# Two sums over all tokens in a linear attention: VectorE adds the token tiles in pairs first, TensorE makes four products for each sum

## The reference, cut to what matters

```
qkv = x @ qkv_w.T + qkv_b                 # 1024 tokens, 16 heads of 8
q, k = sigmoid(q), sigmoid(k)
k_sum = k.sum(tokens)                     # first sum over all tokens, with q_sum
q_sum = q.sum(tokens)
sink_incoming   = 1 / sum((q + EPS) * (k_sum + EPS))
source_outgoing = 1 / sum((k + EPS) * (q_sum + EPS))
k_so_sum = (k * source_outgoing).sum(tokens)   # second sum, with q_si_sum
q_si_sum = (q * sink_incoming).sum(tokens)
conserved_sink   = sum((q + EPS) * (k_so_sum + EPS)) + EPS
conserved_source = clip(sum((k + EPS) * (q_si_sum + EPS)) + EPS, -1, 1)
...
out = (q * sink_incoming) @ (k.T @ (v * softmax(conserved_source) * n)) * sigmoid(conserved_sink)
```

## Time and profile before

| | |
|---|---|
| median of three runs | 2540.83 us |
| the profiled execution | 2537.11 us |
| its span in the trace | 2535.4 us |
| mean granted TensorE clock | 0.962 of full speed |
| TensorE, VectorE, ScalarE, GpSimd busy | 91%, 77%, 65%, 32% of the span |
| first sum (L1850): matmul records, busy | 128, 35.8 us (eight sequences) |
| second sum (L1857): matmul records, busy | 128, 29.8 us |

### The profile page before, as it was taken

One profiled execution on the slowest core, in us unless ns is written; L12 is line 12 of the kernel. 1 busy time (PEld: TensorE's weight loads), 2 busy tenths in 40 slices (PEclk: granted clock), 3 DMA queues, 4 the chain that ended last, 5 costly groups with the idle time before them and its releaser, 6 DMA issues.

```text
span 2535.4 us, 64762 instructions
## 1 busy us (share of the span) xinstructions
PE 2310.6 (91%) x25503; PEld 1658.4 (65%) x25503; DVE 1949.4 (77%) x3307; ACT 1660.4 (65%) x3050; POOL 804.1 (32%) x653
## 2 busy tenths in 40 slices
PE   5989989899898998989989899899998999988998
PEld 3667556675666766667657676566665766666765
DVE  6778877788778887687876878868778687786876
ACT  4866558665586656775577755768457684585845
POOL 2221442315324052241522315313253033530334
PEclk8999999999999999999999999999899999999989
DMA  7110221103111121111211112111121102211022
GB/s 252 51 42 2 96 65 43 42 8 116 39 43 42 44 85 35 47 38 45 88 33 48 34 60 77 35 47 31 63 77 36 46 27 76 69 38 48 18 80 63
DMA packets 99123, 141.34 MB, mean 56 GB/s; under 512 B 11523, under 2 KB 60620, under 8 KB 98316
## 3 DMA queue, kind: packets, MB, share of 16 engines
q1 hardware_dynamic: 90636, 120.41, 15.2%
q0 software_dynamic: 8192, 16.79, 2.3%
HBM read 101.84 MB, written 31.13 MB: 52 GB/s over the span
## 4 chain that ended last, share of the span: by engine, by line
PE 72%; DVE 14%; ACT 6%; issue 6%; POOL 1%; SPq 0%; DVEq 0%; DMA 0%; POOLq 0%; ACTq 0%
PE ps L1727 11%; PE ps L1556 11%; PE ps L1749 10%; PE ps L1764 10%; PE ps L1563 6%; PE ps L1638 5%; DVE neg_max L1225 3%; PE ps L1660 3%; PE ps L1513 2%; DVE ffn L1356 2%; ACT probs L833 2%; PE ps L1577 2%; DVE key_low L989 2%; PE ps L1649 1%; PE ps L1850 1%
## 5 line engine op out<-in xcount | busy, mean ns | idle before, releaser
L1225 DVE TENSOR_REDUCE neg_max<-ps 128x1 f32<-128x1024 f32 x512 | 622.8, 1218 | 84.3 <-PE ps L1727 79.0
L833 ACT ACTIVATE probs<-ps,neg_max 128x1024 f32<-128x1024 f32 x512 | 577.3, 1128 | 53.4 <-DVE neg_max L1225 45.7
L1556 PE MATMUL ps<-shared,w_split 128*128 128x512 f32 x1536 | 471.1, 443 | 18.6 <-ACT ffn L884 11.8
L1749 PEld LDWEIGHTS ps<-ident,probs 64*128 64x128 f32 x8192 | 337.5, 144 | 165.0 <-issue 126.3
L718 POOL TENSOR_TENSOR probs<-ffn,shared 128x512 f32<-128x512 f32 x208 | 287.7, 1383 | 415.3 <-DVE ffn L1356 185.5
L1556 PEld LDWEIGHTS ps<-shared,w_split 128*128 128x128 f32 x1536 | 289.3, 193 | 165.9 <-issue 62.4
L1749 PE MATMUL ps<-ident,probs 64*128 64x64 f32 x8192 | 361.4, 230 | 38.1 <-issue 29.6
L884 ACT ACTIVATE ffn<-ps,room_of_gate 128x512 f32<-128x512 f32 x256 | 175.0, 683 | 274.1 <-PE ps L1556 274.1
L1727 PE MATMUL ps<-shared,query_a 64*128 64x512 f32 x1024 | 267.6, 519 | 82.0 <-ACT probs L833 60.1
L1764 PE MATMUL ps<-probsT,latent 128*32 128x128 f32 x8192 | 326.9, 278 | 3.3 <-DVE o_latent L1218 2.3
L817 ACT COPY probsT<-ps 128x512 f32<-128x512 f32 x512 | 303.5, 593 | 24.0 <-PE ps L1749 23.7
(11 more groups left out here) (232 smaller groups left out, 3534.4 us busy)
## 6 DMA issues: line engine op xcount, KB each, us to landing
w_split<-w_parts SPq DMA_DIRECT2D x132, 256.0 KB, 2.6
shared<-gate_rows SPq DMA_DIRECT2D x64, 512.0 KB, 4.4
y_rows<-probs SPq DMA_DIRECT2D x40, 256.0 KB, 2.2
x_in<-in_x SPq DMA_DIRECT2D x9, 512.0 KB, 4.1
out<-x_mid SPq DMA_DIRECT2D x8, 512.0 KB, 3.2
ffn<-in_gate_up SPq DMA_DIRECT2D x1, 2048.0 KB, 8.6
probsT<-in_gate_up SPq DMA_DIRECT2D x1, 2048.0 KB, 13.2
w_down<-in_down SPq DMA_DIRECT2D x2, 1024.0 KB
```

The lines of the kernel that those rows point to most:

```text
L833: nc.scalar.activation(probs[:, t % 3, :], banks(2 * (t % 2)), ACT.Exp, bias=neg_max[:, t % 4:t % 4 + 1], accum_out=row_sum[:, g % 2, t % ...
L1225: nc.vector.tensor_reduce(neg_max[:, t % 4:t % 4 + 1], banks(2 * (t % 2)), X, ALU.max, negate=True).then_inc(max_ready.sem, 1)
L1556: mm = nc.tensor.matmul(ps[:, bank, :], w_split[:, f % CHUNK_SLOTS, h, k * P:(k + 1) * P], tokens[:, half], start=(part == 0), stop=(part ...
L1749: mm = nc.tensor.transpose(ps[:, turn_bank(t, c), k * HQ:(k + 1) * HQ], probs[rows, t % 3, k * P:(k + 1) * P], ident[rows, rows])
```

## The change

Ahead of each sum VectorE adds token tiles 0 to 3 to tiles 4 to 7 (`folded`, 128 partitions by 4 tiles by 256 columns, in room that is free in this stage), and TensorE streams four tiles instead of eight. The first fold stands right behind VectorE's sigmoid scaling in its unit 2 and waits for that. The second stands behind VectorE's product of unit 10 and waits for both weightings and for the first sum's products. TensorE waits for the folded tiles in place of (first sum) or beside (second sum) what it waited for.

```diff
+FOLD2 = 10
 FLOW_SUMS2 = 12
...
+        folded = room[:, 6 * SEQ:7 * SEQ].rearrange("p (n c) -> p n c", n=NT // 2)
...
+        folded_ready = signal("folded_ready", 2)
...
                         nc.vector.tensor_scalar(qkv[:, :, 0:2 * D], qkv[:, :, 0:2 * D], 0.5, 0.5, ALU.mult, ALU.add
                                                 ).then_inc(qk_ready.sem, 1)
+                        dve.wait_ge(qk_ready.sem, qk_ready.at(b, 1))
+                        nc.vector.tensor_tensor(folded, qkv[:, 0:NT // 2, 0:2 * D], qkv[:, NT // 2:NT, 0:2 * D], ALU.add
+                                                ).then_inc(folded_ready.sem, 1)
...
+                    if u == FOLD2:
+                        dve.wait_ge(weighted_q.sem, weighted_q.at(b, 1))
+                        dve.wait_ge(weighted_k.sem, weighted_k.at(b, 1))
+                        dve.wait_ge(sums_mm.sem, sums_mm.at(b, 1))
+                        nc.vector.tensor_tensor(folded, weighted[:, 0:NT // 2, :], weighted[:, NT // 2:NT, :], ALU.add
+                                                ).then_inc(folded_ready.sem, 1)
...
                     if u == FLOW_SUMS:
-                        pe.wait_ge(qk_ready.sem, qk_ready.at(b, 1))
-                        for n in range(NT):
-                            mm = nc.tensor.matmul(ps[:, 6, 0:2 * D], ones, qkv[:, n, 0:2 * D], start=(n == 0),
-                                                  stop=(n == NT - 1))
+                        pe.wait_ge(folded_ready.sem, folded_ready.at(b, 1))
+                        for n in range(NT // 2):
+                            mm = nc.tensor.matmul(ps[:, 6, 0:2 * D], ones, folded[:, n, :], start=(n == 0),
+                                                  stop=(n == NT // 2 - 1))
                         mm.then_inc(sums_mm.sem, 1)
                     if u == FLOW_SUMS2:
                         pe.wait_ge(weighted_q.sem, weighted_q.at(b, 1))
                         pe.wait_ge(weighted_k.sem, weighted_k.at(b, 1))
-                        for n in range(NT):
-                            mm = nc.tensor.matmul(ps[:, 7, 0:2 * D], ones, weighted[:, n, :], start=(n == 0),
-                                                  stop=(n == NT - 1))
+                        pe.wait_ge(folded_ready.sem, folded_ready.at(b, 2))
+                        for n in range(NT // 2):
+                            mm = nc.tensor.matmul(ps[:, 7, 0:2 * D], ones, folded[:, n, :], start=(n == 0),
+                                                  stop=(n == NT // 2 - 1))
                         mm.then_inc(sums_mm.sem, 1)
```

## The result

| | before | after |
|---|---|---|
| median | 2539.57 us (4 runs, 2535.0 to 2545.32) | 2564.34 us (4 runs, 2562.09 to 2565.21) |
| the profiled execution, its span | 2537.11 us, 2535.4 us | 2563.65 us, 2561.9 us |
| mean granted TensorE clock | 0.962 | 0.956 |
| sigmoid to weighting, mean of eight sequences | 24.44 us | 25.99 us |
| weighting to the reading of the second sum, mean | 5.03 us | 6.91 us |

The ratio is 1.0092 [1.0073, 1.0111]: slower, by 18.5 to 28.2 us. The last three lines of the table are distances between starts in VectorE's timeline and split the whole period of a sequence. The changed kernel's lines: sigmoid L1390, first fold L1393, first sum L1863, weighting L1409, second fold L1415, second sum L1871, its reading L1419.

A forecast was written before the change was run, and what follows sets the result against it. TensorE was 91% busy overall, but between the sums VectorE was busy 22.15 of 23.00 us and the chain ran from VectorE through both sums. Lateness 13 plus clock 10 and 10 gave +33 us on 2540.8: 2574 us, range 2550 to 2592.

The forecast's parts named there:

- First fold, +0.5: First sum: the fold waits for GpSimd's multiply, TensorE starts 2.21 us later and saves 1.67, +0.5 us a sequence.
- The rival of the unheld fold: First sum: GpSimd doesn't hold the fold, the sum starts at 578.50; +25 us in all, 2566 us, chance 0.13.
- Second fold, +1.1: Second sum: the fold is not held, TensorE starts 2.81 us later and saves 1.67; +1.1 us a sequence taken.
- Lateness 8 x 1.6 = +13: Both sums, eight sequences: later starts of 0.5 and 1.1 us pass on to the end, +13 us without the clock.
- The later waits: TensorE's waits behind the second sum, 1.62 and 1.30 us; the forecast had them move along with the delay.
- The clock at the first sum: Behind a 3.1 us pause TensorE's clock falls in all eight sequences: 8 x 2.0 - 6.0 = +10 us.
- The clock at the second sum: Behind a 3.2 us pause TensorE's clock falls in five of eight sequences at 2.0 each, +10 us; bounds 0 and 23.
- The kernel without falls: Rival at both sums: the clock stays up and only the lateness is left, +13 us, 2554 us; chance 0.20.
- the swallowed lateness: Rival: TensorE's two later waits take up the second sum's 1.1 us; 2538 us, not slower, chance 0.10.
- Both folds in cover: Rival at both sums: TensorE reaches them after the folds and the 26.8 us come out; 2514 us, chance 0.02.

The follow-up runs named there:

- e1: The changed kernel with only the first fold, the second sum as before from eight tiles: 2552.57 us, ratio 1.0037.
- e2: The changed kernel with only the second fold, the first sum as before from eight tiles: 2564.27 us, ratio 1.0093.
- e3: The changed kernel, both folds kept, with TensorE making 12 and 11 overwritten products ahead of the waits at the two sums: 2544.15 us, ratio 1.0006.
- e5: The changed kernel with GpSimd waiting for the first fold before its multiply of unit 2: 2549.71 us, ratio 1.004.
- e9: The changed kernel with 12 overwritten TensorE products ahead of the first sum alone: 2554.34 us, ratio 1.0066.
- e7: The changed kernel with the first sum one unit later in TensorE's list (FLOW_SUMS = 5): 2535.31 us, ratio 0.9978.
- e8: The changed kernel with only the first fold, and the first sum one unit later in TensorE's list: 2523.77 us, ratio 0.9935.
- e4: The kernel before, without folds, each sum leaving out tiles 4 to 7: 2532.75 us, ratio 0.9963.

## Why the prediction was right, point by point

- **Direction and mechanism: right.** Both sums start later by more than four products save, both waits end with the fold, and the clock falls behind the longer pauses. e1, e2 and e3 show the parts.
- **First fold, +0.5 with GpSimd's multiply ahead of it: right.** 2.168 us long and 3.47 from sigmoid to sum, where the working had 3.47; e3 has +0.51. e5 shows that the multiply is the cause: the fold takes 1.226 us without it. The rival of the unheld fold falls with it. The Trainium skill (Advanced Engine Details and Errata, VectorE Performance Modes) says that VectorE's two-port instructions and GpSimd's block each other, and lists no two-port mode for a two-operand `tensor_tensor`; that such an instruction would therefore not wait is the working's reading, and the measurement decides against it: the fold was held for 0.94 us. The Trainium skill's other page (SBUF — State Buffer, Who interferes with whom) says that a VectorE instruction with two SBUF inputs contends with a GpSimd instruction that reads SBUF; with that this trace agrees, by the same 0.94 us.
- **Second fold, +1.1: right.** 1.210 us and unheld; TensorE's pause 3.30 us for the 3.2 of the working; e3 has +1.18.
- **Lateness 8 x 1.6 = +13, all of it passing on: right.** 8 x (0.51 + 1.15) = 13.3 in the changed kernel. The later waits swallowed nothing: reading to next sigmoid moved by -0.17 us a sequence, and the two waits of the earlier trace rows, 1.62 and 1.30 us, are 1.28 and 1.30 in sequence 1:

```profile
625.46 1.67 PE L1569 MATMUL ps<-shared,w_split 128*128 128x512 f32 x6 [1.28 <-ACT ffn L888]
...
629.28 1.02 PE L1522 MATMUL ps<-xT_first,w_beta 128*16 128x512 f32 x2 [1.30 <-DVE query_a L984]
```

- **The clock at the first sum, falls in all eight, +10: right in number, a little dear.** Eight falls cost 8 x (25.99 - 24.20) = 14.3 us, 1.8 each for 2.0; less the 6.0 of before, +8.3. One reading in the working is wrong: the first sum of sequence 0 did not run wholly at the lower clock, which ended 5.9 us into its 6.62.
- **The clock at the second sum, five falls at 2.0, +10: the mis-sized term.** Six fell, at 0.99 us each, +5.9. The count was one too low and the price twice too high, and it is luck that the two errors lie against each other. A fall of the first sum was taken as the price for one at the second. But the price is what of the sum lies behind the beginning of the fall, and five of the six began 0.65 to 1.23 us into a sum of 1.96. That the dearer price can occur is seen in the sixth, in sequence 2, and in e2 and e9: 1.8.
- **The sum.** 13.3 + 8.3 + 5.9 - 1.2 + 0.3 is, unrounded, 26.5 us of span, for 33 predicted. The time, 2564.34 us, lies inside the range and 9.7 under the forecast: 6.5 by the terms above, 1.8 since the medians differ by 24.8 and the two profiled spans by 26.5, and 1.3 since the median of before came down from 2540.8 to 2539.6.
- **The rivals.** The kernel without falls, 2554 by the prediction, exists as e3 and took 2544.15: the rival left in the falls that the kernel before has already, 6.0 us, and they go too. The other 4 us stay open; by the ratio e3 is 1.5 us over the kernel before, by the traces 5.7, where 13.5 - 6.0 would be 7.5. The unheld fold exists as e5: 8.2 us less from sigmoid to weighting, where the prediction had 7.5. Of the swallowed lateness nothing is seen. Both folds in cover was not reached even with the sum moved, since VectorE has no time to spare there (e7, e8), and e4 shows that of the 26.8 us behind it 9 are had by the ratio, and 16 by its trace.

## What to carry to other kernels

Work moved off the busiest engine gains nothing where that engine waits at that very place for the engine that takes the work on: see in the timeline who ends the wait, and count the start, not the instructions. Ahead of a wait that cannot be shortened, ask which independent work of the same queue can go first: one constant here gave 1.0%, by filling TensorE's pause, keeping its clock, giving VectorE work during the sum and taking a VectorE product out of the way of a GpSimd multiply. Price a fall of the clock by where it begins, not by a fall elsewhere. And see how the traced execution lies among the others before its sums are set beside a median.

## What the runs showed of the hardware beyond the expectation

- What the filled pauses give does not add. Keeping TensorE busy ahead of the first sum gave 6.6 us (not clear of noise), ahead of the second nothing, ahead of both 22.
- Behind the bias products on 8 rows and one down product, the clock fell at short pauses and stayed up at longer ones: 0.35, 0.64 and 0.76 us in the three sequences of e4 in which it fell, 0.47 to 0.98 in the five in which it did not. Whether the pause or the products ahead of it brought the fall is not shown.
- A GpSimd multiply that had waited during the sigmoid went ahead of the fold, which stood directly behind the sigmoid on VectorE, in 8 of 8 sequences: it was issued 1.06 us before the sigmoid's end and ended 1.08 us before the fold, which took 2164 to 2168 ns.
